# Second attention, scalar engine: the copy of turned probabilities and the exponential of the next step change places

## The reference, cut to what matters

```python
Q = jnp.einsum('bqd,hdk->hbqk', q, w_qs)          # q: 16 x 100 x 256, H = 16, KD = 64
K = jnp.einsum('bsd,hdk->hbsk', k, w_ks)          # k = v = ctx: 16 x 361 x 256
V = jnp.einsum('bsd,hdv->hbsv', v, w_vs)
scores = jnp.einsum('hbqk,hbsk->hbqs', Q, K) / scale
attn = jax.nn.softmax(scores, axis=-1)            # per head 100 x 361
out = jnp.einsum('hbqs,hbsv->hbqv', attn, V)
lin = cat @ W_o.T + b_o                           # cat: the 16 heads side by side
```

## Time and profile before

| | before |
|---|---|
| median of 3 runs | 1683.36 us (1679.73 to 1685.15) |
| profiled execution, its time | 1681.74 us |
| its span in the trace | 1679.9 us, granted clock 0.899 |
| TensorE matmuls busy | 1311.7 us (78%) |
| VectorE busy | 869.0 us (52%) |
| ScalarE busy | 810.1 us (48%) |
| GpSimd busy | 308.4 us (18%) |

### The profile page before, as it was taken

How to read it: one execution, slowest core, us unless ns; L and a number is a source line. 1 busy time by engine, 2 the same in 40 slices (tenths; PEclk the granted TensorE clock), 3 DMA queues, 4 the chain that set the end, 5 groups by cost and what they waited for, 6 DMA issues and landing times. The chain is left out here.

```text
span 1679.9 us, 35318 instructions
## 1 busy us (share of the span) xinstructions
PE 1311.7 (78%) x10632; PEld 1041.5 (62%) x10633; DVE 869.0 (52%) x2918; ACT 810.1 (48%) x2219; POOL 308.4 (18%) x337
## 2 busy tenths in 40 slices
PE   3699999984089998059999999999999973049970
PEld 2576676664078888057787878787878753026650
DVE  3466666664035544446665656665665656302223
ACT  3588778773044543136554555555545544013320
POOL 2333333310700000711000000000000000430016
PEclk9899999995589999569999999999999995579995
DMA  5811000000232320220000000000000000822113
GB/s 138 346 29 27 26 26 26 27 2 0 78 139 100 134 104 26 74 83 11 21 11 11 10 10 10 10 10 10 10 10 0 1 1 0 319 60 66 62 58 107
DMA packets 42626, 92.25 MB, mean 55 GB/s; under 512 B 10205, under 2 KB 30877, under 8 KB 39261
## 3 DMA queue, kind: packets, MB, share of 16 engines
q1 hardware_dynamic: 32468, 77.37, 13.6%
q0 software_dynamic: 8192, 13.15, 2.8%
q10 hardware_dynamic: 1872, 0.68, 0.3%
HBM read 66.18 MB, written 24.97 MB: 54 GB/s over the span
## 5 line engine op out<-in xcount | busy, mean ns | idle before, releaser
L507 ACT ACTIVATE b_prob<-b_prob,b_low 100x361 f32<-100x361 f32 x256 | 155.6, 608 | 108.0 <-DVE b_low L596 108.0
L364 PE MATMUL b_ps_p<-b_context_part,b_wk_part 128*128 128x362 f32 x768 | 157.7, 342 | 0.0
L1046 ACT ACTIVATE a_prob<-a_prob,a_low 100x361 f32<-100x361 f32 x256 | 154.2, 605 | 4.4 <-DVE a_low L1164 4.4
L515 ACT COPY b_prob_t<-b_ps_t 128x300 f32<-128x300 f32 x256 | 103.8, 406 | 104.2 <-PE b_ps_t L420 101.3
L370 PE MATMUL b_ps_p<-b_wv_part,b_context_part 128*128 128x512 f32 (+1 forms) x576 | 151.6, 406 | 0.0
L596 DVE CUSTOM_DVE_ANT_0 b_prob<-b_ps_s,b_mask_bias 100x361 f32<-100x361 f32 x256 | 121.3, 532 | 45.3 <-PE b_ps_s L410 30.0
L1164 DVE CUSTOM_DVE_ANT_0 a_prob<-a_ps_s,a_mask_bias 100x361 f32<-100x361 f32 x256 | 121.5, 532 | 34.8 <-PE a_ps_s L947 34.8
L420 PE MATMUL b_ps_t<-ident,b_prob 100*128 100x100 f32 x768 | 117.1, 261 | 22.1 <-ACT b_prob_t L515 21.5
L1054 ACT COPY a_prob_t<-a_ps_t 128x300 f32<-128x300 f32 x256 | 97.7, 409 | 67.7 <-PE a_ps_t L957 64.8
L364 PEld LDWEIGHTS b_ps_p<-b_context_part,b_wk_part 128*128 128x128 f32 x768 | 124.6, 189 | 0.3 <-issue 0.2
L420 PEld LDWEIGHTS b_ps_t<-ident,b_prob 100*128 100x128 f32 x768 | 78.1, 141 | 66.3 <-issue 52.4
(11 more groups left out here) (205 smaller groups left out, 2530.5 us busy)
## 6 DMA issues: line engine op xcount, KB each, us to landing
rows_in<-zero SPq DMA_DIRECT2D x16, 512.0 KB, 13.9
w<-in_c_fc SPq DMA_DIRECT2D x8, 1024.0 KB, 6.3
w<-in_c_proj SPq DMA_DIRECT2D x8, 1024.0 KB, 4.9
f_w<-in_W SPq DMA_DIRECT2D x2, 4096.0 KB
a_context<-in_ctx SPq DMA_DIRECT2D x16, 361.0 KB, 3.6
b_context<-in_ctx SPq DMA_DIRECT2D x16, 361.0 KB
f_xe<-rows_in SPq DMA_DIRECT2D x8, 512.0 KB, 3.9
rows_out<-f_ye SPq DMA_DIRECT2D x8, 512.0 KB, 3.0
```

The lines of the kernel that those rows point to most:

```text
L364: ins = nc.tensor.matmul(bank[:, 0:LN2], w_parts["k"][a][:, k, t * P:(t + 1) * P], cx_parts[s][b][:, k, :], start=m == 0, stop=m == DK * l ...
L507: nc.scalar.activation(prob[0:S, k, 0:L], prob[0:S, k, 0:L], ACT.Exp, bias=low[0:S, k:k + 1], scale=-1.0, accum_out=total[0:S, k:k + 1]).t ...
L515: nc.scalar.copy(pt[:, k % PAIR_PT, :], ps_t[:, 0:KT_N * S]).then_inc(pt_ready.sem, 1)
L1046: nc.scalar.activation(prob[0:S, k, 0:L], prob[0:S, k, 0:L], ACT.Exp, bias=low[0:S, k:k + 1], scale=-1.0, accum_out=total[0:S, r:r + 1]).t ...
```

## The change

In the second attention ScalarE's list for a step had, for each m, the exponential of head m of step p and behind it the copy of turned head m of step p-1, then the taking of unit m-1. Now the copy stands first and the exponential behind it. The instructions, their number and all waits of the single instruction are the same.

```diff
                     for m in range(4):
+                        if lag:
+                            keep_turned(*lag, m)
                         if p < STEPS:
                             exp(i, 4 * p + m)
-                        if lag:
-                            keep_turned(*lag, m)
                         if m:
                             for args in units[m - 1:m]:
                                 take(*args, sched, i)
```

## The result

The changed kernel takes 1726.15 us, median of 4 runs (1723.77 to 1732.21), against 1681.99 before, median of 4: ratio 1.0267, 95% interval 1.0234 to 1.0300. It is 44 us slower where 26 were forecast, and lies above the range. The direction and the places of the waits were right. The size was not, because the forecast had no term for a fall of TensorE's clock behind the largest new wait.

What follows compares the result with a forecast made beforehand. TensorE's list was taken as the bound (busy 592.3 of 618.0 us). Inner iterations +22.6, step-0 gains -5.1, first iteration +0.5, last +7.5 gave 25.5 us longer: 1708 us, own range 1700 to 1716, 1698 to 1721 with rival 1.

Steps and rivals of the forecast that it cites:

- the largest new wait: End of step 2: score's g = 1 waits for the out_t copy; 2.64 us lost, hole grown to 3.0 us.
- turn 1 in time in steps 1, 2, 5, 6: Copy 0 starts when turn 0 ends, so turn 1 stops waiting: 0.16 us gained per step, 0.64 per iteration.
- one spacing in step 7: Step 7: turn 2 runs where turn 1 was, a gain of one turn-to-turn spacing, 1.05 us.
- copy 3 ahead of exponential 3 costs through inversion 3: After turn 3: copy, exponential, inversion run in chain; VectorE's next operation starts 1.72 us after turn 3's start.
- The losses at the heads of steps 1, 2 and 3: Score's g = 1 waits for keep_group behind inversion 3: 1.21, 0.4 and 2.64 us, together 4.25 per iteration.
- W's share: End of step 2: W's four VectorE operations, 1.79 us, precede keep_group; without W the loss is 1.2 instead of 2.64.
- the bank of unit 2 in step 4: Step 4: unit 5 needs unit 2's bank, whose rounding stands behind an exponential; 0.59 us lost.
- The sum of the waits: Whole kernel: inner iterations 22.6, less step-0 gains 5.1, plus first iteration 0.5 and last 7.5: 25.5 us longer.
- rival 1: Clock falls in the new hole at step 2's end: seven holes, 11 us more, 1719 us; chance 0.09.
- a sign of being wrong: Forecast called itself wrong if the clock over the stage fell under 1.00 before its last microseconds.
- the price of the fall: Each of seven new holes costs 3 us at half clock, 1.5 us each, 11 more.
- step 0's gain: Step 0 after the loop's jump back, five times: between nothing and 1.5 us gained, taken as 0.95.

Runs made afterwards that it cites:

- the filling: Changed kernel with 28 needless TensorE transposes ahead of g = 0 in step 3, to fill the 2.9 us hole: 1716.1 us, ratio 1.019.
- the out_t copy moved: Kernel with copies 0 to 2 first, VectorE's out_t copy (keep_group) also moved ahead of inversion 3: 1666.2 us, ratio 0.992.

## Why the prediction was wrong in size

**Right, and shown.** That TensorE's list is the bound and ScalarE's order matters only through it. The gains: turn 1 in time in steps 1, 2, 5, 6, one spacing in step 7 (0.87 net of 0.85 forecast). That copy 3 ahead of exponential 3 costs through inversion 3: copy 3 first alone is 1740 us, copies 0 to 2 first is 1668. The losses at the heads of steps 1, 2 and 3 (holes of 1.21, 0.26 and 2.91 us), W's share in the last (1.28 us without it), and the bank of unit 2 in step 4 (+0.57 of 0.59). The sum of the waits: 25.5 us forecast, of which 1.4 lie in step 7 of the last iteration, behind the stage as measured; with the clock held up by the filling, the stage is 22.7 us longer than before, 1.0 of it for the filling of the first iteration, where the hole was short.

**Wrong: no term for the clock.** This is the step that failed. The sum is made of waits at full clock. The prediction named the fall of the clock in the new hole as rival 1 and gave it 0.09, on the argument that holes of up to 1.4 us did nothing before and that the work around is dense. That argument can't carry a step from 1.4 to 3.0 us. Dense work around the hole didn't help: in the changed kernel the clock fell at all seven holes (six of 2.9 us, one of 2.6), and its mean from 850 to 1300 us is 0.96. The prediction had named that as a sign of being wrong. The Trainium skill (TensorE: Matmul & The Clock Gate, Part 1: The HAM clock gate), which says that an idle stretch halves the clock and sustained work gives it back, was cited as speaking for the rival. The traces agree in the main: the granted clock fell to 0.50 at holes of 2.9 us and came back after 5.9 us of work. But one hole of 2.9 us in six passed at full clock when copy 3 alone stood first, and one of 1.7 us brought it down in two iterations of six.

**Wrong: the price of the fall.** It was set at 3 us of half clock per hole, from the one fall at the stage's end, 1.5 us each, and would have given 1719, still 7 too low. The rows after show some 6.8 us at 0.50 in five of the seven iterations, which cost 2.7 to 3.0 us each, and some 3.4 us in the other two, at 1.5 to 1.6 (step 3 against the length that the waits alone make). In the last iteration the clock was at 0.50 once more, for some 10 us from 1395.8 us, in the short steps 5 and 6 (step 6 took 11.7 us, and 9.2 with the hole filled). Together some 20.7 us of the profiled execution (the 19.7 that the filled kernel is faster, and the 1.0 that its filling costs in the first iteration), where 11 were priced.

The stage of the profiled execution is 42.4 us longer than before: 22.7 with the clock held up, and 19.7 more without. That the medians differ by 44.2 us is no check of this to the microsecond: the two profiled executions differ by 50.5, of which 6.2 lie outside the second attention (1062.8 us before, 1069.0 after; 1060.0 to 1072.6 in the other kernels), and it is by luck that the medians come so near.

**Too low: step 0's gain,** 0.95 against 1.2 to 1.6 us: in the iteration of the table copy 0 now starts 0.59 us after turn 0 (921.23 to 921.82), nearly as soon as elsewhere (0.52), so ScalarE was back from its jump almost in time, which the rows before couldn't show. Over five iterations this is 2.0 us. It is most of what the waits are below the forecast: 24.1 us were forecast for the stage as measured, and 22.7 less the filling's 1.0 is 21.7.

**Open.** Why the clock's price differs between holes of one length (no fall, some 3.4 us or some 6.8 us at 0.50) and between executions of one kernel (1723.8 to 1732.2 us) is not settled.

## What to carry to other kernels

When two operations of an in-order engine change places, look at the last pair of a group, not at the average: what is queued behind its result on the next engine, and which wait on the bound engine that feeds. Here the same exchange was worth 15 us for the first three copies and cost 57 us for the fourth (medians against the kernel before). And when a forecast opens an idle stretch on TensorE longer than any that the trace shows at full clock, price the half clock behind it as part of the sum, by the longest fall that can be found, not as a side case.

The best kernels are those with copies 0 to 2 ahead of the exponential and copy 3 behind: 1668 us, or 1666 with the out_t copy moved too, 0.8 to 0.9% faster than before.

## What the runs showed of the hardware that was not expected

After 2.9 us without a matmul the granted clock stood at 0.50 for some 6.8 us in all, although TensorE worked through nearly all of it (949.6 to 955.5 us). The same hole brought it down in all six inner iterations of the changed kernel, and in five of six when copy 3 alone stood first. After 1.7 us it fell in two of six inner iterations of one execution, and after 1.2 us in none of them. In the last iteration of the changed kernel, where TensorE was busy 2.8 of the 5 us before it, it fell with no hole over 1.1 us in the 15 us before. Twenty-eight needless transposes in the idle stretch, 2.4 us of work, made the kernel 10 us faster (1726.2 to 1716.1 us, medians).
